# First edge stage of a four-layer graph network: node sums of 128 rows, the last layer applied per node, selections and counts on GpSimd

## The reference

```
h = softplus(concat(x[r], edge_attr) @ W1 + b1)      # 128 -> 128
h = softplus(h @ W2 + b2)                            # 128 -> 128
out = h @ W3 + b3                                    # 128 -> 64
agg = segment_sum(out, r);  result x + agg
```

## Time and profile before

| | |
|---|---|
| Median of 3 runs | 7905.99 us (7904.19 to 7910.43) |
| The profiled execution, own time | 7911.44 us |
| its span, first to last instruction | 7909.9 us |
| PE busy | 6871.9 us, 87% |
| DVE busy | 5452.2 us, 69% |
| ACT busy | 3670.3 us, 46% |
| POOL busy | 5106.9 us, 65% |
| Mean granted TensorE clock | 0.889 |

### The profile page before, as it was taken

One profiled execution on the slowest core, in us unless ns is written; L12 is line 12 of the kernel. 1 busy time (PEld: TensorE's weight loads), 2 busy tenths in 40 slices (PEclk: granted clock), 3 DMA queues, 4 the chain that ended last, 5 costly groups with the idle time before them and its releaser, 6 DMA issues.

```text
span 7909.9 us, 179277 instructions
## 1 busy us (share of the span) xinstructions
PE 6871.9 (87%) x37306; PEld 3483.7 (44%) x37467; DVE 5452.2 (69%) x18163; ACT 3670.3 (46%) x6211; POOL 5106.9 (65%) x5691
## 2 busy tenths in 40 slices
PE   6999999967777777777767999999999989998998
PEld 5777777633333333333323444444444444444443
DVE  7888888857888888878865777777777743332222
ACT  5999999845555555555643333333333301110000
POOL 4333333337777777777766777777777657663777
PEclk9999999976676767667668999999999999998999
DMA  4333333243332333333322222222222256665765
GB/s 125 97 97 96 96 97 96 83 154 98 91 98 91 96 95 95 95 95 93 97 76 57 60 61 62 61 60 61 61 61 60 51 165 173 167 169 155 200 194 160
DMA packets 785297, 810.21 MB, mean 102 GB/s; under 512 B 246570, under 2 KB 590487, under 8 KB 785111
## 3 DMA queue, kind: packets, MB, share of 16 engines
q1 hardware_dynamic: 586999, 629.91, 25.0%
q0 software_dynamic: 147776, 160.99, 10.3%
q10 hardware_dynamic: 50400, 17.87, 0.9%
HBM read 581.59 MB, written 227.43 MB: 102 GB/s over the span
## 4 chain that ended last, share of the span: by engine, by line
PE 58%; DVE 14%; issue 12%; POOL 8%; ACT 2%; DMA 2%; DVEq 2%; SPq 1%; ACTq 0%; POOLq 0%; another core or an unknown queue 0%
PE ps L2547 8%; PE ps L2386 7%; PE ps L2185 6%; PE ps L2203 5%; POOL zone L1030 5%; PE ps L2210 4%; PE ps L2552 4%; PE ps L2378 4%; PE ps L2350 3%; POOL zone L1070 3%; DVE zone L1657 2%; DVE zone L1374 2%; DVE zone L1659 2%; PE ps L2405 2%; DMA zone<-tab_msg,idx 2%
## 5 line engine op out<-in xcount | busy, mean ns | idle before, releaser
L1030 POOL DMA_INDIRECT zone<-tab_msg,idx x1664 | 1903.8, 1144 | 526.5 <-issue 450.9
L1030 POOL DMA_INDIRECT zone<-tab_u,idx x1664 | 1582.6, 951 | 597.2 <-issue 478.7
L2024 ACT ACTIVATE zone<-ps 128x792 fp8e4<-128x792 f32 x1600 | 1258.6, 829 | 878.4 <-PE ps L2350 870.0
L2350 PE MATMUL ps<-zone 128*128 128x396 bf16 x3200 | 1116.7, 449 | 352.8 <-ACT zone L2024 182.7
L1374 DVE TENSOR_TENSOR zone<-ps,zone 128x512 f32<-128x512 f32 x1664 | 1064.0, 686 | 365.5 <-PE ps L2378 230.4
L2185 PE MATMUL ps<-zone 128*128 128x64 f32 (+1 forms) x6656 | 825.9, 278 | 252.5 <-DMA zone<-tab_msg,idx 247.6
L1659 DVE TENSOR_SCALAR zone<-tT,zone 128x392 bf16<-128x392 f16 x3200 | 1023.2, 320 | 0.0
L2185 PEld LDWEIGHTS ps<-zone 128*128 128x128 f32 (+1 forms) x6656 | 727.3, 189 | 393.3 <-issue 374.9
L2386 PE MATMUL ps<-zone,w_bas 128*64 128x512 f32 x3328 | 899.5, 619 | 0.0
L2547 PE MATMUL ps<-zone 128*128 128x512 fp8e4 x3332 | 841.8, 382 | 24.9 <-DMA zone<-adj 14.6
L1657 DVE TENSOR_SCALAR zone<-tT,zone 128x128 bf16<-128x128 f16 x3200 | 803.6, 251 | 3.4
(11 more groups left out here) (324 smaller groups left out, 10386.0 us busy)
## 6 DMA issues: line engine op xcount, KB each, us to landing
zone<-adj SPq DMA_DIRECT2D x238, 768.0 KB
adj<-zone SPq DMA_DIRECT2D x200, 784.0 KB
zone<-in_dst_row SPq DMA_DIRECT2D x832, 128.0 KB, 2.6
zone<-in_ea_T SPq DMA_DIRECT2D x416, 128.0 KB, 2.5
zone<-src_lin SPq DMA_DIRECT2D x3264, 0.5 KB
zone<-adj SPq DMA_DIRECT2D x34, 896.0 KB
tab_msg<-zone SPq DMA_DIRECT2D x104, 256.0 KB, 2.1
zone<-tab_msg,idx POOLq DMA_INDIRECT x1664
```

The lines of the kernel that those rows point to most:

```text
L1030: nc.gpsimd.indirect_dma_start(out=gat(e, u)[:, k, :], out_offset=None, in_=table, in_offset=bass.IndirectOffsetOnAxis(ap=idx[:, u, k:k + ...
L2024: nc.scalar.activation(staging[m % 2][:, :, at_ * 2 * WN:(at_ + 1) * 2 * WN].rearrange("p b (w d) -> p w b d", w=2), pair_[:, :, 0:CX].rea ...
L2350: mm(bank(4 + w % 4)[:, 0:CX], hot_lo[w % HOTS], hot_hi[w % HOTS], start=True, stop=True) \
```

## The change

- ScalarE takes exp and ln(1 + that) straight from the first layer's value; VectorE forms min(that, 40) and then the maximum with the value itself, in one instruction. The absolute value goes. The same short form serves the second layer.
- The second layer's bias is added by VectorE (`bias_stage`), from PSUM into an SBUF buffer `pre2`, with `b_l02`, a copy of the bias in every partition. The bias matmul goes, and with it the split of the bias, its round trip through memory and the waits for it. The clip on VectorE goes.
- `acc` is 128 rows high and collects the sums of the second layer: banks 4 to 7 take them in turn, and VectorE adds 128 x 64 instead of 65 x 64, at lag 7 instead of 8. `to_acc` and `move` go.
- The selection of odd chunks stays on VectorE; that of even chunks is made on GpSimd by four comparisons of 128 x 64 (`match_even`), from `rel_now`, a copy made once an iteration.
- The counts are kept by lane on GpSimd: `lane_cnt`, in float16, 128 x nodes, lies where `h` was, is cleared by one memset before the loop, and gets two dependent 128 x 64 additions per chunk (`count`) in place of one. GpSimd now loads the eight window starts per iteration.
- In the message stage, `weigh_sums` multiplies, for each group of 512 nodes, `W3` with `acc` (float32) and the three bf16 parts of `b3` with `lane_cnt`, ScalarE copies the 65 rows back (`settle_sums`), and `turn_sums` follows. Five such steps come before the first messages, where four transposes did.

The core of the diff, with eight columns of indentation taken off:

```diff
-acc = sb("acc", [D + 1, NP])
+acc = sb("acc", [P128, NP])
...
+lane_cnt = home("h").bitcast(FP16)
...
-moved = home("moved").rearrange("p (s e) -> p s e", s=2)
+b3_parts = home("moved").bitcast(BF16)[:, 0:3 * (D + 2)].rearrange("p (n c) -> p n c", n=3)
...
-sel_sum = ring_mem[:, 8 * CE + 4 * W:8 * CE + (4 + SL) * W].rearrange("p (s c) -> p s c", s=SL)
+rel_now = ring_mem[:, 8 * CE + 4 * W:8 * CE + 4 * W + RING * TL]
+pre2 = [ring_mem[:, n * CE:(n + 1) * CE] for n in (9, 12)]
...
+    pool.wait_ge(first_turned, NG)
+    pool.wait_ge(residual, len(PARTS))
+    nc.gpsimd.memset(home("h"), 0.0).then_inc(cnt_added, 1)
+    wait_stores(pool, AFTER[0])
...
+        pool.wait_ge(windowed, p + 1)
+        pool.sem_inc(pool_turn, 1)
...
+        def match_even(it, u):
+            pool.wait_ge(agg_done, done(g, it, u, SL))
+            pool.sem_inc(pool_turn, 1)
+            for k in range(TL):
+                ins = nc.gpsimd.tensor_scalar(sel(0, u)[:, k, :], iota_w[:, :], rel_now[:, u * TL + k:u * TL + k + 1], None, ALU.is_equal)
+            ins.then_inc(sel_even, 1)
+
+        def halve(it, u):
+            if u % 2 == 0:
+                pool.wait_ge(sel_even, done2(g2, it, u // 2))
+            else:
+                pool.wait_ge(sel_built, done(g, it, u))
+            pool.wait_ge(cnt_added, g3 + it * (2 * RING) + (2 * u + 1))
             nc.gpsimd.tensor_tensor(sel_half[:, u % 2], sel(0, u)[:, 0:2, :], sel(0, u)[:, 2:4, :], ALU.add) \
                 .then_inc(sel_halved, 1)
...
-                                    ALU.add).then_inc(sel_summed, 1)
+            into = lane_cnt[:, bass.ds(base, W)]
+            for n in range(2):
+                if n == 1:
+                    pool.wait_ge(cnt_added, g3 + it * (2 * RING) + (2 * u + 2))
+                pool.sem_inc(pool_turn, 1)
+                nc.gpsimd.tensor_tensor(into, into, sel_half[:, u % 2, n, :], ALU.add).then_inc(cnt_added, 1)
...
             load_piece(it)
+            bases = bases_of(mybir.EngineType.Pool, it * RING)
+            pool.sem_inc(pool_turn, 1)
+            nc.gpsimd.tensor_copy(rel_now, rel[:, bass.ds(it * (RING * TL), RING * TL)]).then_inc(rel_copied, 1)
+            pool.wait_ge(rel_copied, first + it + 1)
+            pool.sem_inc(pool_turn, 1)
             for u in range(RING):
                 if u == RING // 2:
                     split_piece(it)
-                halve(it, u, None)
-                add_up(it, u, None)
+                if u % 2 == 0:
+                    match_even(it, u)
+                halve(it, u)
+                count(it, u, bases[u])
...
+        order(nc.vector.tensor_copy(b3_parts[:, 0, 0:D + 1], b_l0o[:, :]))
+        order(nc.vector.tensor_tensor(b_l0o[:, :], b_l0o[:, :], b3_parts[:, 0, 0:D + 1], ALU.subtract))
+        order(nc.vector.tensor_copy(b3_parts[:, 1, 0:D + 1], b_l0o[:, :]))
+        nc.vector.tensor_tensor(b3_parts[:, 2, 0:D + 1], b_l0o[:, :], b3_parts[:, 1, 0:D + 1], ALU.subtract)
...
-    ADD_LAG = {0: 8, 1: 4, 2: 7}
+    ADD_LAG = {0: 7, 1: 4, 2: 7}
...
-        def soft_of_size(it, u, _):
-
+        def soft1_stage(it, u, _):
             dve.wait_ge(softened1, done_of(2, g, it, u, 1))
             dve.wait_ge(mm2_done, done(g, it, u, 2))
-            nc.vector.scalar_tensor_tensor(out=hid1[:, u % 2, :], in0=bank(u % 2), scalar=0.0,
-                                           in1=soft1[:, u % 2, :], op0=ALU.max, op1=ALU.add) \
-                .then_inc(hid1_ready, 1)
-
-        return [(3, soft_of_size),
-                (4, clip(mm2_done, hid2_ready, clipped2, soft2, 2)),
-                (5, soft(hid2_ready, softened2, hid_summed, None, soft2, hid2, 2)),
+            nc.vector.scalar_tensor_tensor(out=hid1[:, u % 2, :], in0=soft1[:, u % 2, :], scalar=CLIP,
+                                           in1=bank(u % 2), op0=ALU.min, op1=ALU.max).then_inc(hid1_ready, 1)
+
+        def bias_stage(it, u, _):
+            dve.wait_ge(mm2_done, done(g, it, u))
+            dve.wait_ge(hid2_ready, done(g, it, u, 2))
+            nc.vector.tensor_tensor(pre2[u % 2].rearrange("p (k c) -> p k c", k=TL),
+                                    bank(2 + u % 2).rearrange("p (k c) -> p k c", k=TL),
+                                    b_l02[:, :].unsqueeze(1).to_broadcast([P128, TL, H]), ALU.add) \
+                .then_inc(biased2, 1)
+
+        def soft2_stage(it, u, _):
+            dve.wait_ge(softened2, done_of(2, g, it, u, 1))
+            dve.wait_ge(agg_done, done(g, it, u, 2))
+            nc.vector.scalar_tensor_tensor(out=hid2[:, u % 2, :], in0=soft2[:, u % 2, :], scalar=CLIP,
+                                           in1=pre2[u % 2], op0=ALU.min, op1=ALU.max).then_inc(hid2_ready, 1)
+
+        def sel_odd(it, u, _):
+            if u % 2 == 1:
+                dve.wait_ge(agg_done, done(g, it, u, SL))
+                dve.wait_ge(sel_halved, done(g, it, u, SL))
+                at_ = rel[:, bass.ds((it * RING + u) * TL, TL)]
+                nc.vector.tensor_tensor(sel(0, u), at_.unsqueeze(2).to_broadcast([P128, TL, W]),
+                                        iota_w[:, :].unsqueeze(1).to_broadcast([P128, TL, W]), ALU.is_equal) \
+                    .then_inc(sel_built, 2)
+
+        return [(3, soft1_stage),
+                (4, bias_stage),
+                (5, soft2_stage),
                 (0, selT_stage(0, p, slice(D, P128), 3)),
-                (4, sel_stage(0, p)),
-                (8, add_stage(0, p, D + 1, (6, 7)))]
+                (4, sel_odd),
+                (ADD_LAG[0], add_stage(0, p, H, (4, 5, 6, 7)))]
...
-        def soften(clipped, softened, buf):
+        def soften(made, ready, softened, buf, src):
             def stage_(it, u, _):
-                act.wait_ge(clipped, done(g, it, u))
-                nc.scalar.activation(buf[:, u % 2, :], buf[:, u % 2, :], ACT.Exp).then_inc(softened, 1)
+                act.wait_ge(made, done(g, it, u))
+                act.wait_ge(ready, done(g, it, u, 2))
+                nc.scalar.activation(buf[:, u % 2, :], src[u % 2], ACT.Exp).then_inc(softened, 1)
                 act.wait_ge(softened, done_of(2, g, it, u, 0))
                 nc.scalar.activation(buf[:, u % 2, :], buf[:, u % 2, :], ACT.Ln, bias=1.0).then_inc(softened, 1)
             return stage_
...
+        chunk_loop(act, [(2, soften(mm1_done, hid1_ready, softened1, soft1, [bank(0), bank(1)])),
+                         (4, soften(biased2, hid2_ready, softened2, soft2, pre2))])
+
+    def settle_sums(n):
+        if n < NG:
+            act.wait_ge(sums_weighed, n + 1)
+            nc.scalar.activation(acc[0:D + 1, n * GN:(n + 1) * GN], bank(n % 2)[0:D + 1, :], ACT.Copy) \
+                .then_inc(sums_settled, 1)
+
     def lift_rows(j):
         act.wait_ge(rows_turned, j + 1)
...
+    for n in range(5):
+        settle_sums(n)
...
+        for n in range(j + 7 if j else 5, j + 8):
+            settle_sums(n)
...
+            if e == 0 and u % 2 == 0:
+                pe.wait_ge(sel_even, done2(gp, it, u // 2))
+            else:
+                pe.wait_ge(sel_built, done(ga, it, u))
+            pe.wait_ge(agg_added, done(ga, it, u, len(banks)))
...
-            pe.wait_ge(hid2_ready, done(g, it, u, 2))
+            pe.wait_ge(biased2, done(g, it, u, 2))
             out_ = bank(2 + u % 2).rearrange("p (k c) -> p k c", k=TL)
-            mm(out_, ones_b[:, :], bpart[:, :].unsqueeze(1).to_broadcast([3, TL, H]), start=True, stop=False)
             for k in range(TL):
-                last = mm(out_[:, k, :], hid1[:, u % 2, k * P128:(k + 1) * P128], w_l0m[:, :],
-                          start=False, stop=k == TL - 1)
+                last = mm(out_[:, k, :], hid1[:, u % 2, k * P128:(k + 1) * P128], w_l0m[:, :], start=True, stop=True)
...
-            (1, mm1), (3, mm2), (6, to_acc),
+            (1, mm1), (3, mm2),
             (5, sum_stage(0, p, H, lambda u: hid2[:, u % 2, :].rearrange("p (k c) -> p k c", k=TL),
-                          hid2_here, (4, 5), hid_summed))])
+                          hid2_here, (4, 5, 6, 7)))])
...
+    def weigh_sums(j):
         if j >= 2:
             pe.wait_ge(x_added, j - 1)
+        cols = slice(j * GN, (j + 1) * GN)
+        out_ = bank(j % 2)[0:D + 1, :]
+        mm(out_, w_l0o[:, :], acc[:, cols], start=True, stop=False)
+        for n in range(3):
+            last = mm(out_, b3_parts[:, n, 0:D + 1], lane_cnt[:, cols], start=False, stop=n == 2)
+        last.then_inc(sums_weighed, 1)
+
+    def sums_step(n):
+        if n < NG:
+            weigh_sums(n)
+        if 1 <= n <= NG:
+            turn_sums(n - 1)
...
-    for j in range(4):
-        turn_sums(j)
+    pe.wait_ge(cnt_added, P * (2 * CH) + 1)
+    pe.sem_inc(pe_turn, 1)
+    for n in range(5):
+        sums_step(n)
...
-        for n in range(j + 6 if j else 4, min(j + 7, NG)):
-            turn_sums(n)
+        for n in range(j + 7 if j else 5, j + 8):
+            sums_step(n)
```

(42 more changed lines are left out.)

66 lines of the change are left out of this document (11 added, 55 removed).

## The result

The changed kernel takes **8055.18 us** (median of 4 runs, 8052.9 to 8060.88) against 7908.21 (7904.19 to 7915.01): ratio 1.0186, 95% interval 1.0168 to 1.0204. It is slower; 7840 was forecast, and the range ended at 7945.

What follows compares the result with a forecast made beforehand. TensorE bounds the kernel now at 3.44 us per chunk; after the change GpSimd and the shared ports would, at 3.15. Edge stage -121, message stage +55, ends 0: -66 from 7906 gives 7840 us, range 7722 to 7945.

Steps and rivals of the forecast that it cites:

- The comparison: GpSimd, even chunks: four added comparisons at 0.20 us each, between a memset's 0.14 and a two-input addition's 0.32.
- The rest of GpSimd's sum: GpSimd per eight chunks: 1.38 us per odd chunk, waits 0.10, split 4.99, loop's end 1.29, loads and copy 1.1.
- Meetings with VectorE: Edge stage: shared SBUF ports make GpSimd lose 2.9 us to softplus and 0.3 to selections per eight chunks.
- The wait at the split: Edge stage: TensorE stands some 2 us per iteration before its sum, waiting for GpSimd's even comparisons; 0.25 us per chunk.
- Rival D: Edge stage: TensorE's clock falls after the split wait, 0.33 us per chunk on top, 3.48, 7978 us; chance 0.05.
- Rival C: Edge stage: GpSimd's comparisons at 0.32 us make 3.39 per chunk, 7940 us; with dearer meetings 3.68, 8061; chance 0.20.
- TensorE, 2.88 us a chunk: Edge stage: without the bias matmul (0.32 us) and `to_acc` (0.24), TensorE falls from 3.44 to 2.88 us per chunk.
- VectorE, 2.85: Edge stage: VectorE's instructions, with the selection only every other chunk, together take 2.85 us per chunk.
- Rival B: Edge stage: TensorE binds at 2.90 us per chunk if meetings cost little and comparisons are near 0.14; 7736 us; chance 0.30.
- Message stage, +55: Message stage: 26 groups of added matmuls cost 49 us on busy TensorE, plus 6 before the first messages.
- The ends: Start: GpSimd's memset holds VectorE up to 5 us; the pipeline's drain takes 5 us less; they cancel.
- The second edge stage: Second edge stage and the rest, same code: forecast difference 0.

Runs made afterwards that it cites:

- e3: Changed kernel with every selection built on VectorE as before the change, no comparisons on GpSimd; sums, weighing and counts stay as changed: 7733.51 us.
- the experiment on the ports: Changed kernel with VectorE's second softplus reading its unbiased input from PSUM, so only one input is in SBUF; the second matmul waits for that read: 7924.53 us.
- e1: Changed kernel with GpSimd's comparisons for the next even chunk queued ahead of the odd chunk's halving, and so of the split: 7980.52 us.
- e5: Changed kernel with GpSimd building only every fourth chunk's selections, those of chunk 4 queued ahead of the last halving and the split: 7862.65 us.
- e6: As e3, but GpSimd begins its wide memset only once VectorE has cast the windowed columns: 7730.72 us.

## Why the prediction was wrong

**The comparison, 0.20 us, bounds 0.14 to 0.32.** This is the step that failed. It measured (1.84 - 0.17)/4 = 0.42 us, above the upper bound. The prediction took a comparison for nearer to a memset, "reads one tensor", and took the two-input addition for a ceiling. Neither row was the same operation; the comparison also takes a number per partition, and it came out dearer than the addition of the same size (0.32). With the wait, an even chunk added 1.84 instead of 0.90 us: 3.8 of the 5.6 us between 25.2 forecast and 30.8 measured. That the comparisons decide the sign, e3 shows: without them on GpSimd the time is 7733.51 us, with them 8055.18.

**The rest of GpSimd's sum.** Halving and both counts 1.47 instead of 1.38, eight times: 0.7. The waits for its own result are 0.25 and 0.18 us where 0.10 was taken. Split 5.6 instead of 4.99, meetings included. Start and end of the loop 2.4 as forecast. Meetings with VectorE took some 2.8 us of the 3.2 forecast, an estimate from what comparisons, halvings and split took over their undisturbed times, and the experiment on the ports agrees. New, and in no term: the wait for VectorE's late selection, 1.2 us in the mean and up to 1.7.

**The wait at the split, 2 us** became 4.6 to 5.0. Its working was right in kind: place, waiting line and frequency are as forecast. But from the halving at 713.37 to the end of the comparisons some 8.9 us pass, not 8, two chunks of TensorE give only 5.3 us of slack, not 6, and GpSimd comes late already. That the wait is no mere shadow of the length, e1 and e5 show: with the comparisons ahead of the split the time fell by 75 and by 133 us.

**Rival D, the clock, chance 0.05,** happened, though not as a cause by itself: it was set against 2 us of standstill, "less than 3.07", and the standstill was 4.6. Its price was right (2.7 us forecast; 5.28 - 2.65 measured), but most of it seems to be hidden, as GpSimd is behind anyway: only GpSimd's wait of up to 1.69 us can come from it. No run changes the clock alone, so this is argued.

**Rival C** is the one that came, beyond its own upper price for the comparison: with 0.42 its sum gives 25.2 + 16 x 0.22 = 28.7 us, 3.59 a chunk, and with the prediction's +55 already 8023 us; the terms above make the rest. Its chance of 0.20 was too small because the price was bounded by rows of other operations. That its upper time, 8061, lies so near the measured 8055 is luck: the step passed its 3.68 us by 0.14, some 59 us in all, and the second edge stage gave 46 back and the message stage with the drain 11.

**TensorE, 2.88 us a chunk.** Smooth chunks took 2.65: the second matmul's eight parts take 0.89 instead of 1.09 without the bias matmul ahead of them, the sum 0.84 instead of 0.89. **VectorE, 2.85** with half of the selections: 2.90 with all. Rival B's mechanism, an edge stage bound elsewhere, thus needs GpSimd out of the way; e3 comes near its time (7736) with 3.05 us instead of 2.90, by luck: the edge stage took some 61 us more than at 2.90, the second edge stage gave 34 us that nobody had counted, and the message stage with the drain cost 33 instead of 50.

**Message stage, +55:** +42 from the first to the last of it; a group's three half-precision products take 0.65 us, not 0.96. **The ends:** the first matmul came 6 us later, 5 forecast, and the memset had some 4 of them (e6), from one instruction held for 5.40 us; the drain gave 3 instead of 5. **The second edge stage** was put at nothing and gave 46. The Trainium skill, SBUF — State Buffer, section "Who interferes with whom", speaks of VectorE instructions with two SBUF inputs. The trace agrees for these (GpSimd's comparison 526 ns beside such a softplus, 481 beside one that reads PSUM). It also shows one with a single SBUF tensor held, the 5.40 us beside the memset.

## What to carry to other kernels

Price an operation that the trace doesn't show from above by more than the nearest row: if the forecast turns over within twice that price, its sign isn't known. Before work goes to an idle engine, look at what stands ahead of it in that engine's queue (here 5.6 us of split) and at how soon the busy engine needs it; of a queue that is both full and in the wrong order, mending one alone gives little. An engine's idle share isn't its room: GpSimd was the limit at 74% busy, most of the rest being waits for its own results and issues.

## What was not expected of the hardware

A comparison of 128x64 numbers with one number per partition takes 0.42 us on GpSimd from one start to the next, and an addition of the same size to `lane_cnt` 0.29 to 0.31 undisturbed, one of two float32 tensors 0.32: fewer numbers read, more time.

The second edge stage, the same code and data, has two forms, and one run lay between them. Groups of GpSimd by line, the kernel before and then after (1664 gathers each: busy us, mean ns, idle):

```profile
L1030 POOL DMA_INDIRECT zone<-tab_msg,idx x1664 | 1903.8, 1144 | 526.5 <-issue 450.9
```
```profile
L1049 POOL DMA_INDIRECT zone<-tab_msg,idx x1664 | 1856.9, 1116 | 526.3 <-issue 430.4
```

The idle time is the same, and 46.9 us more are spent in the gathers. A timeline of GpSimd, the kernel before, shows them:

```profile
2499.32 2.83 POOL L1030 DMA_INDIRECT zone<-tab_msg,idx  x1 [0.31 <-issue]
2502.46 1.00 POOL L1030 DMA_INDIRECT zone<-tab_msg,idx  x1 [0.30 <-DVE idx L1305]
2503.77 2.88 POOL L1030 DMA_INDIRECT zone<-tab_msg,idx  x1 [0.30 <-issue]
2506.95 0.94 POOL L1030 DMA_INDIRECT zone<-tab_msg,idx  x1 [0.30 <-issue]
```

143 of the 1664 last over 1.6 us before, 96 after; counted by their place in the loop of 32 gathers (from 0), there are 39 at places 12, 18, 19 and 24 before and none after. It hid 46 us of the change's cost in the comparison of the two kernels; whoever weighs a change to one stage by the time of the whole should look at the stages that were not changed, too.
